# Graph attention with residual layernorm on one core: work units of one pair for both rings, or of one quad for one ring

## The chip, the core and the metric

The kernel runs on one core of one Trainium2 chip. The metric is the device time of one execution in microseconds (us); each kernel is run several times and the median is taken. Engines: TensorE (PE; its weight loads are PEld), VectorE (DVE), ScalarE (ACT), GpSimd (POOL), and SyncE (SP), which only issues DMAs here.

## The reference

```python
def reference(x, adj, W, a):          # x 8192x128 f32, adj 8192x8192 int32 (0/1, sparse, with diagonal)
    Wh = (h @ W.T).reshape(n, 4, 32).transpose(1, 0, 2)
    score_src = einsum('knd,kd->kn', Wh, a[:, :32])[:, :, None]
    score_dst = einsum('knd,kd->kn', Wh, a[:, 32:])[:, None, :]
    e = leaky_relu(score_src + score_dst, 0.2)
    e = where(adj == 0, -inf, e)
    alpha = softmax(e, axis=-1)
    h_prime = einsum('kij,kjd->kid', alpha, Wh)     # 4 heads of 32
    return layernorm(x + h_prime.transpose(1, 0, 2).reshape(n, 128))
```

## The kernel before

The exponential of a leaky ReLU is a product of one factor per row and one per column, and which of two such products holds depends only on whether the sum of the two scores is above zero. So no exponential is taken per edge. For each head a byte mask says where the sum is above zero; "edge and mask" selects the columns for the steep branch (values G), "edge exclusive-or (edge and mask)" those for the flat branch (values F). Both masks are fed to TensorE as fp8 weights, 128 columns by 128 rows at a time, and 66 columns of values (32 of data and a one for the denominator, twice: a coarse and a fine fp16 part) flow past them.

Rows are done in 16 groups of 512 (GROUPS, ROWS), the 8192 columns in 64 blocks of 128, two blocks to a pair: 32 pairs to a group (PAIRS), 512 in all. The four heads lie in two "rings" (RINGS) of two. For pair k:

- ACT and POOL make the masks of pair k (L513 to L519, L411 to L417): 4 comparisons of 128x1024, each for two groups at once (this group for one head, the next group for the other). ACT takes 2 or 3 of the 4 (2.25 on average), POOL the rest (1.75). In group 0 the masks of the other heads are made as well, in 128x512 comparisons; in the last group comparisons are 128x512. Before pair k both engines wait for the products and the exclusive or of pair k-5 (NS = 5 places, L407, L415 to L416 and their ACT twins).
- PE transposes the edges of pair k+2 into one of three PSUM banks (`transpose_edges`, L742, four transposes, AHEAD = 2, NT = 3).
- DVE does the and (`take_step`, L630) for both rings at once, 128x1024 int32 words, one operand from PSUM and one from SBUF; then the exclusive or (`take_rest`, L638) of pair k-1, the same size. The exclusive or waits until the products two before it are done (NL = 2).
- PE does 32 products with the and of pair k (`add_step`), the four transposes of pair k+2, and 32 products with the exclusive or of pair k-1 (`add_rest`), all at L754. They accumulate over a whole group in five PSUM banks; a small matmul with zeros opens a bank (L765) and another closes it (L769).

At the end of a group g the sums are finished while group g+1 runs. ACT copies the five banks to SBUF (`take_sums`, L492) after its comparisons for pair 4 of the next group (SUMS = 4). PE can open a bank for group g+1 only after its copy. POOL combines the sums in eight parts (`close`, L356 to L380) after its comparisons of the pairs in CLOSING. DVE does the reciprocal of the denominator and the layernorm statistics in `finish` (L656 to L678) from pair 16 on, POOL the inverse deviation (L384), DVE the shift (L678, `scalar_tensor_tensor` of 128x4 with both inputs in SBUF), ACT the normalisation (L498) after pair 30, and SP stores the rows.

POOL also issues the loads of edges (L337): 4 loads of 256 KB for every chunk of 8 pairs, one each after its comparisons of pairs 2, 3, 4, 5 of every eight (EDGE_UNITS), for the next chunk. The order on each engine is the order written out in its block; nothing is planned by a scheduler.

## Time and profile before

| | us |
|---|---|
| median of 3 runs | 1487.32 (1482.68 to 1493.78) |
| the profiled execution | 1484.16 |
| span in its profile | 1482.3 |
| PE, DVE, ACT, POOL busy | 1204.4, 1307.4, 1333.5, 1328.0 |

The span runs from the first to the last instruction on the core, so 1.9 us of the profiled execution lie around it. "Busy" is the time in which an engine works on at least one instruction. "Idle before" a group of instructions is the time in which their engine had nothing to do just before them, with what ended it. "issue" means that the engine waited for nothing that the profile shows.

### The profile page before, as it was taken

How to read it: one execution, taken by the hardware profiler on the slowest of the kernel's cores; microseconds unless marked ns; L12 is line 12 of the kernel's file. 1: busy time of each engine (PE TensorE's matmuls, PEld its weight loads, DVE VectorE, ACT ScalarE, POOL GpSimd, SP SyncE). 2: the span in 40 equal slices, each digit the busy share in tenths (PEclk: the TensorE clock that was granted, in tenths of full speed). 3: DMA queues.
4: the chain of work that ended last, by engine and by line, in shares of the span. 5: the costliest groups of instructions: out<-in, count | busy, mean ns of one | idle time of the engine just before them, and what ended most of it. 6: DMA issues, size and time to landing. Idle time of an engine off the chain costs nothing.

```text
span 1482.3 us, 77436 instructions
## 1 busy us (share of the span) xinstructions
PE 1204.4 (81%) x35173; PEld 1177.2 (79%) x35173; DVE 1307.4 (88%) x1422; ACT 1333.5 (90%) x1456; POOL 1328.0 (90%) x1371
## 2 busy tenths in 40 slices
PE   7047679898888889888897989889887989888985
PEld 7036669897888889788897989888887879888984
DVE  6966669899898999999798999989999889989995
ACT  2799999999999999999999999999999999999753
POOL 1788879999999999999999999999999999999854
PEclk9569989999999999999999999999999999999997
DMA  8203555657757675656746675666657665675740
GB/s 162 57 30 34 50 73 53 62 80 67 94 47 95 55 97 57 64 80 67 91 45 94 61 72 74 64 87 57 93 51 97 58 61 77 67 80 49 73 46 24
DMA packets 55842, 101.65 MB, mean 69 GB/s; under 512 B 5721, under 2 KB 18393, under 8 KB 55513
## 3 DMA queue, kind: packets, MB, share of 16 engines
q0 software_dynamic: 36864, 67.13, 52.0%
q1 hardware_dynamic: 18648, 29.56, 6.2%
q8 instruction: 277, 4.54, 1.2%
q14 instruction: 53, 0.43, 0.1%
HBM read 293.67 MB, written 4.33 MB: 201 GB/s over the span
## 4 chain that ended last, share of the span: by engine, by line
PE 45%; POOL 19%; issue 14%; ACT 11%; DVE 5%; POOLq 0%; DVEq 0%; ACTq 0%
PE bank L754 40%; POOL kept L341 14%; ACT kept L465 10%; PE bank L742 5%; DVE kept L630 3%; POOL edge L337 2%; DVE rest L638 1%; DVE shift L678 1%; POOL late L371 1%; POOL y L380 0%; ACT late L492 0%; POOL late L367 0%; POOL late L358 0%; POOL late L364 0%; POOL late L374 0%
## 5 line engine op out<-in xcount | busy, mean ns | idle before, releaser
L465 ACT ACTIVATE kept<-s_two,sd 128x1024 uint8<-128x1024 f32 (+1 forms) x1152 | 1196.5, 1116 | 87.0 <-DVE rest L638 50.1
L341 POOL TENSOR_SCALAR kept<-s_two,sd 128x1024 uint8<-128x1024 f32 (+1 forms) x896 | 967.8, 1091 | 37.0 <-DVE rest L638 19.6
L630 DVE TENSOR_TENSOR kept<-bank,kept 128x1024 int32<-128x1024 int32 x512 | 621.3, 1216 | 111.1 <-PE bank L742 79.1
L754 PE MATMUL bank<-G,kept 128*128 128x66 f16 x16384 | 600.9, 194 | 106.6 <-issue 57.9
L638 DVE TENSOR_TENSOR rest<-kept,bank 128x1024 int32<-128x1024 int32 x512 | 618.5, 1209 | 33.6 <-PE bank L754 33.4
L754 PEld LDWEIGHTS bank<-G,kept 128*128 128x128 fp8e4 x16384 | 544.4, 98 | 120.4 <-issue 64.4
L754 PE MATMUL bank<-F,rest 128*128 128x66 f16 x16384 | 595.5, 194 | 46.2 <-issue 45.7
L754 PEld LDWEIGHTS bank<-F,rest 128*128 128x128 fp8e4 x16384 | 555.4, 98 | 51.0 <-issue 50.7
L742 PE MATMUL bank<-identb,edge 128*128 128x128 bf16 x2048 | 201.9, 222 | 17.2 <-issue 9.0
L337 POOL DMA_DIRECT2D edge<-in_adj x256 | 151.5, 593 | 16.0 <-DMA kept<-in_x 16.0
L742 PEld LDWEIGHTS bank<-identb,edge 128*128 128x128 bf16 x2048 | 125.0, 98 | 24.1 <-issue 10.0
L765 PE MATMUL bank<-zeros,identb 128*128 128x2 bf16 x80 | 13.6, 169 | 80.5 <-DVE kept L630 51.3
L765 PEld LDWEIGHTS bank<-zeros,identb 128*128 128x128 bf16 x80 | 8.2, 102 | 81.7 <-issue 75.3
L341 POOL TENSOR_SCALAR kept<-y,sd 128x512 uint8<-128x512 f32 x30 | 31.6, 1053 | 19.5 <-DMA late<-sT_scratch 10.1
L356 POOL TENSOR_TENSOR late<-late 128x528 f32<-128x528 f32 x16 | 17.9, 1120 | 28.4 <-ACT late L492 28.4
L492 ACT COPY late<-bank 128x462 f32<-128x462 f32 (+1 forms) x80 | 34.1, 510 | 7.9 <-PE bank L769 7.9
L498 ACT ACTIVATE y<-y,shift,rstd 128x128 f32<-128x128 f32 x64 | 26.2, 480 | 13.1 <-DVE shift L678 13.1
L678 DVE SCALAR_TENSOR_TENSOR shift<-mv,rstd 128x4 f32<-128x4 f32 x16 | 34.0, 2123 | 1.1 <-POOL rstd L384 1.1
L341 POOL TENSOR_SCALAR kept<-late,sd 128x512 uint8<-128x512 f32 x30 | 21.7, 722 | 10.8 <-PE bank L754 7.3
L374 POOL TENSOR_TENSOR late<-late,rden 128x512 f32<-128x512 f32 x16 | 16.9, 1056 | 11.1 <-DVE rden L659 10.9
L384 POOL TENSOR_TENSOR rstd<-mv,half_t 128x4 f32<-128x4 f32 x16 | 16.7, 1043 | 11.2 <-DVE mv L673 11.2
L440 ACT COPY late<-bank 128x512 f32<-128x512 f32 x16 | 9.4, 586 | 18.9 <-PE bank L704 18.9
(77 smaller groups left out, 405.4 us busy)
## 6 DMA issues: line engine op xcount, KB each, us to landing
edge<-in_adj POOLq DMA_DIRECT2D x256, 256.0 KB, 5.3
s_two<-sT_scratch SPq DMA_DIRECT2D x30, 512.0 KB, 6.5
kept<-in_x SPq DMA_DIRECT2D x16, 256.0 KB, 6.5
y<-in_x SPq DMA_DIRECT2D x16, 256.0 KB, 7.5
out<-y SPq DMA_DIRECT2D x16, 256.0 KB, 7.2
s_two<-sT_scratch SPq DMA_DIRECT2D x2, 256.0 KB, 6.5
y<-sT_scratch SPq DMA_DIRECT2D x1, 256.0 KB, 3.7
late<-sT_scratch SPq DMA_DIRECT2D x1, 256.0 KB, 4.8
```

The source lines that it names most:

```text
L337: nc.gpsimd.dma_start(edge[:, c % NC, b], adj_v[c // (PAIRS // CP), c % (PAIRS // CP), :, b // E, b % E]).then_inc(edge_loaded[c % NC], 16)
L341: return nc.gpsimd.tensor_scalar(out, scores, STEEP, d_steep[:, j, h:h + 1], ALU.mult, ALU.add)
L356: nc.gpsimd.tensor_tensor(low, low, sums_F[:, :, HC:FC], ALU.add).then_inc(low_set, 1)
L465: return nc.scalar.activation(out, scores, ACT.Sigmoid, scale=STEEP, bias=d_steep[:, j, h:h + 1])
L492: nc.scalar.copy(late[:, b * USED:b * USED + n], acc[b][:, 0:n]).then_inc(acc_act, 1)
L498: last = nc.scalar.activation(y[:, b], y[:, b], ACT.Identity, scale=rstd[:, b:b + 1], bias=shift[:, b:b + 1])
L630: nc.vector.tensor_tensor(kept[:, :, both(k, k)[0]], edgeT[k % NT], kept[:, :, both(k, k)[0]], ALU.bitwise_and).then_inc(step_set, 1)
L638: nc.vector.tensor_tensor(rest[:, k % NL], kept[:, :, both(k, k)[0]], edgeT[k % NT], ALU.bitwise_xor).then_inc(rest_set, 1)
L678: nc.vector.scalar_tensor_tensor(shift[:, :], mv[:, :, 0], -1.0, rstd[:, :], ALU.mult, ALU.mult).then_inc(shift_set, 1)
L742: last = nc.tensor.transpose(edgeT16[k % NT][:, b * P:(b + 1) * P], edge16[:, c % NC, b, k % CP * P:(k % CP + 1) * P], identb[:, :])
L754: last = nc.tensor.matmul(acc[k][:, col:col + BC], matrices[h][:, b * P:(b + 1) * P, e], values[:, t * E + e, h].rearrange("p s c -> p (s ...
L765: nc.tensor.matmul(acc[k][:, USED:USED + 2], identb[:, :], zeros[:, :], start=True, stop=False, skip_group_check=True)
```

## The change

The unit of DVE's work becomes one ring of four column blocks (a quad, QUADS = 16 to a group) instead of both rings of two column blocks. A unit keeps its size: 128x1024 for the and and the exclusive or, 4 comparisons, 32 products. Unit k belongs to quad k // 2 and ring k % 2. What else changes:

- Order on DVE for each quad: and, and, exclusive or, exclusive or. On PE: eight transposes of quad q+2, then 32 + 32 products of the two ands, then 32 + 32 of the two exclusive ors. A transposed quad fills its bank; still three banks.
- NS = 3 quads: comparisons for unit k wait for unit k-6.
- The sums are read from PSUM by DVE: per group three `tensor_scalar` and three `tensor_tensor` adds (fine part scaled and added to the coarse), and three `tensor_reduce`. Banks 0 and 1 are closed ahead of the last two exclusive-or products and read before DVE's first and of the next group; banks 2 to 4 are read between its second and and its first exclusive or. ACT's copies go.
- Row factors: numerator and denominator share one of them, so a single `ratio` replaces alpha and beta. POOL's closing has 4 parts instead of 8; in the last group they are done by DVE.
- The shift goes from DVE (`scalar_tensor_tensor`) to POOL (a product of 128x4), with the negated mean from a DVE `tensor_scalar`.
- Loads of edges after units 1 to 4 of every eight instead of 2 to 5.

```diff
-    EDGE_UNITS = (2, 3, 4, 5)
+    EDGE_UNITS = (1, 2, 3, 4)
+    CQ = CP // U
-    NS = 5
-    PLACES = PAIRS + NS
+    NS = 3
+    PLACES = QUADS + NS
-    WORDS = ROWS * E // 4
+    WORDS = ROWS * E // 4 * U
-        CLOSING = (4, 6, 8, 10, 12, 14, 18, 20)
-        SUMS, FINISH, DEVIATION, SCALED = 4, 16, 26, 30
+        CLOSING = (7, 9, 17, 19)
+        FINISH, DEVIATION, SCALED = 12, 28, 31
...
                 if part == 0:
-                    pool.wait_ge(acc_act, done((g + 2) * BANKS))
-                    nc.gpsimd.tensor_tensor(low, low, sums_F[:, :, HC:FC], ALU.add).then_inc(low_set, 1)
+                    pool.wait_ge(acc_taken, done((g + 2) * BANKS))
+                    nc.gpsimd.tensor_tensor(sum_F, sum_F, per_row(ratio[:, g * IB:(g + 1) * IB, :], HC), ALU.mult).then_inc(low_set, 1)
                 elif part == 1:
-                    nc.gpsimd.tensor_scalar(sums_G[:, :, HC:BC], sums_G[:, :, HC:BC], 1.0 / LOW, None, ALU.mult).then_inc(top_set, 1)
+                    pool.wait_ge(low_set, g + 1)
+                    nc.gpsimd.tensor_tensor(sum_G, sum_G, sum_F, ALU.add).then_inc(top_set, 1)
...
                 nc.gpsimd.tensor_tensor(rstd[:, :], mv[:, :, 1], half_t[:, :], ALU.pow).then_inc(rstd_set, 1)
+                pool.wait_ge(rstd_set, g + 1)
+                nc.gpsimd.tensor_tensor(shift[:, :], minus_mean[:, :], rstd[:, :], ALU.mult).then_inc(shift_set, 1)
...
-                    if k >= NS:
-                        pool.wait_ge(step_done, k - NS + 1)
-                        pool.wait_ge(rest_set, k - NS + 1)
+                    q, r = quad_and_ring(k)
+                    if q >= NS:
+                        pool.wait_ge(step_done, k - RINGS * NS + 1)
+                        pool.wait_ge(rest_set, k - RINGS * NS + 1)
...
+            def take_sums(g, b):
+                dve.wait_ge(acc_done, g * BANKS + b + 1)
+                first, end = b * PER_BANK, b * PER_BANK + sums_in(b)
+                unit_of = acc[b][:, 0:(end - first) * BC].rearrange("p (k s c) -> p k s c", s=BP, c=HC)
+                n_G = max(0, min(end, CHUNKS) - first)
+                if end > CHUNKS:
+                    at = first + n_G - CHUNKS
+                    last = nc.vector.tensor_reduce(sum_F[:, at:end - CHUNKS], unit_of[:, n_G:].rearrange("p k s c -> p k c s"), AX.X, ALU.add)
+                if n_G > 0:
+                    nc.vector.tensor_scalar(sum_G[:, first:first + n_G], unit_of[:, 0:n_G, 1], 1.0 / LOW, None, ALU.mult).then_inc(small_taken, 1)
+                    dve.wait_ge(small_taken, g * BANKS_G + b + 1)
+                    last = nc.vector.tensor_tensor(sum_G[:, first:first + n_G], unit_of[:, 0:n_G, 0], sum_G[:, first:first + n_G], ALU.add)
+                last.then_inc(acc_taken, 1)
...
-                for t in range(PAIRS):
-                    take_step(pair_no(g, t))
-                    if t > 0:
-                        take_rest(pair_no(g, t - 1))
-                    if t >= FINISH and t % 2 == 0:
+                for t in range(0, PAIRS, RINGS):
+                    k = pair_no(g, t)
+                    if t == 0 and g > 0:
+                        take_sums(g - 1, 0)
+                        take_sums(g - 1, 1)
+                    for r in range(RINGS):
+                        take_step(k + r)
+                    if t == 0 and g > 0:
+                        for b in range(2, BANKS):
+                            take_sums(g - 1, b)
+                    for r in range(RINGS):
+                        take_rest(k + r)
+                    if t >= FINISH:
                         next(closing, None)
...
-                for t in range(PAIRS):
-                    k = pair_no(g, t)
-                    add_step(g, t)
-                    if t > 0:
-                        pe.wait_ge(rest_set, k)
-                    if k + AHEAD < GROUPS * PAIRS:
-                        transpose_edges(k + AHEAD)
-                    if t > 0:
-                        add_rest(g, t - 1)
+                for t in range(0, PAIRS, RINGS):
+                    q = pair_no(g, t) // RINGS
+                    if q + AHEAD < GROUPS * QUADS:
+                        transpose_edges(q + AHEAD)
+                    for r in range(RINGS):
+                        add_step(t + r)
+                    if t + RINGS == PAIRS:
+                        for b in range(CHUNKS // PER_BANK):
+                            close_bank(b)
+                    for r in range(RINGS):
+                        add_rest(t + r)
+                for b in range(CHUNKS // PER_BANK, BANKS):
+                    close_bank(b)
```

In the setup five small DVE operations (three of 128x256 for alpha and beta, a copy, a negation) and their two scalings make way for one `tensor_scalar`, and two exponentials on ACT for one.

## Rows read from the trace of the kernel before

**Rows 1.** Windows: length, busy PE, PEld, DVE, ACT, POOL, PE clock, DMA share, GB/s

```profile
209.29:1384.63 1175.34, 1021.63 (x30604) 1002.86 (x30605) 1079.72 (x1063) 1115.10 (x1135) 1130.00 (x1134) 0.98 0.64 72
1384.63:1464.30 79.67, 72.54 (x2178) 71.16 (x2178) 72.91 (x75) 45.00 (x73) 47.88 (x66) 0.98 0.45 47
```

**Rows 2.** Who waited for whom in 209.29 to 1384.63 (us, times, longest us)

```profile
PE bank L754 <- issue: 96.5, 74, 3.5
DVE kept L630 <- PE bank L742: 55.5, 38, 6.8
DVE rest L638 <- PE bank L754: 32.3, 34, 2.5
PE bank L765 <- ACT late L492: 29.0, 14, 6.7
PE bank L754 <- DVE kept L630: 20.8, 22, 2.1
```

**Rows 3.** Timeline of PE, one place (start us, us; bracket: idle before)

```profile
725.07 0.64 PE L754 MATMUL bank<-G,kept 128*128 128x66 f16 x16 [2.14 <-issue]
...
726.74 1.12 PE L754 MATMUL bank<-G,kept 128*128 128x66 f16 x32
727.70 0.38 PE L742 MATMUL bank<-identb,edge 128*128 128x128 bf16 x4
727.92 0.77 PE L754 MATMUL bank<-F,rest 128*128 128x66 f16 x20
```

**Rows 4.** DMA queue of instructions, whole span: packets, MB, share of 16 engines

```profile
q8 instruction: 277, 4.54, 1.2%
```

**Rows 5.** Groups of instructions, 209.29 to 1384.63: busy us, mean ns | idle before

```profile
L678 DVE SCALAR_TENSOR_TENSOR shift<-mv,rstd 128x4 f32<-128x4 f32 x14 | 33.7, 2404 | 0.0
L492 ACT COPY late<-bank 128x462 f32<-128x462 f32 (+1 forms) x71 | 30.3, 510 | 0.0
L358 POOL TENSOR_SCALAR late<-late 128x528 f32<-128x528 f32 x14 | 21.8, 1560 | 0.0
L364 POOL TENSOR_TENSOR late<-late 128x528 f32<-128x528 f32 x14 | 15.9, 1137 | 0.4
L356 POOL TENSOR_TENSOR late<-late 128x528 f32<-128x528 f32 x14 | 15.7, 1121 | 16.6 <-ACT late L492 16.6
L367 POOL TENSOR_TENSOR late<-late,alpha 128x528 f32<-128x528 f32 x14 | 15.4, 1103 | 0.4
```

**Rows 6.** Timeline of DVE: around the shift of one group, and the shift of group 14

```profile
441.84 2.41 DVE L678 SCALAR_TENSOR_TENSOR shift<-mv,rstd 128x4 f32<-128x4 f32 x1
444.17 1.21 DVE L630 TENSOR_TENSOR kept<-bank,kept 128x1024 int32<-128x1024 int32 x1
445.31 1.20 DVE L638 TENSOR_TENSOR rest<-kept,bank 128x1024 int32<-128x1024 int32 x1
...
1450.46 0.15 DVE L678 SCALAR_TENSOR_TENSOR shift<-mv,rstd 128x4 f32<-128x4 f32 x1
```

**Rows 7.** Groups of instructions by form, whole span: nearest kin of the added operations

```profile
L604 DVE TENSOR_TENSOR late<-bank,G 128x396 f32<-128x396 f32 x21 | 11.7, 557 | 0.0
L555 DVE TENSOR_REDUCE wh_part<-bank 128x1 f32<-128x256 f32 x32 | 13.1, 411 | 0.0
L384 POOL TENSOR_TENSOR rstd<-mv,half_t 128x4 f32<-128x4 f32 x16 | 16.7, 1043 | 11.2 <-DVE mv L673 11.2
```

**Rows 8.** Setup, timeline of DVE: one of the operations that go

```profile
38.79 0.42 DVE L572 SCALAR_TENSOR_TENSOR beta<-alpha,beta 128x256 f32<-128x256 f32 x1
```

**Rows 9.** Timeline of the tail after the last bank is closed

```profile
1464.14 0.17 PE L769 MATMUL bank<-zeros,identb 128*128 128x2 bf16 x1
...
1475.20 0.87 DVE L664 BATCH_NORM_STATS2 stats<-y 128x6 f32<-128x128 f32 x4 [2.42 <-POOL y L380]
```

**Rows 10.** Edge loads: last load of a chunk; landing times in 209.29 to 1384.63

```profile
715.57 0.60 POOL L337 DMA_DIRECT2D edge<-in_adj  x1
...
DMA to landing us min/median/max: 4.9/5.3/8.5
```

More of the change, by code:

```diff
@@ L484, in _ @@
             second_part(UNITS - 1)
-            def take_sums(g):
-                act.wait_ge(var_set, done(g))
-                for b in range(BANKS):
-                    n = sums_in(b) * BC
-                    act.wait_ge(acc_done, g * BANKS + b + 1)
-                    nc.scalar.copy(late[:, b * USED:b * USED + n], acc[b][:, 0:n]).then_inc(acc_act, 1)
             def normalise(g):
@@ L693, in _ @@
+            nc.vector.tensor_tensor(rows_y, rows_y, sum_G[:, :, 0:D_OUT], ALU.add).then_inc(sum_set, 1)
+            for _ in closing:
                 pass
@@ L746, in add_pair @@
[L746 to L759 removed]
+                if q >= NT:
+                    pe.wait_ge(rest_set, RINGS * (q - NT + 1))
@@ L770, in close_bank, with two_heads @@
                                  skip_group_check=True).then_inc(acc_done, 1)
-            def by_head(g, k):
-                older, newer = places(k)
-                kept_first = both(k, k)[1]
+            def two_heads(g, q):
+                older, newer = places(q)
+                kept_first = both(q, q)[1]
                 two = [(newer, int(kept_first)), (older, int(not kept_first))]
-                two = two if g % 2 == 0 else two[::-1]
-                return [(r, place, side) for r in range(RINGS) for place, side in two]
@@ L791, in group @@
[L791 to L802 removed]
+                return two if g % 2 == 0 else two[::-1]
```

245 lines of the change are left out of this document (118 added, 127 removed).

## The prediction

> **What bounds the kernel now.** I read the share of busy time first, then cut the span at the openings of the accumulation banks, since these mark the groups. Group 0 ends with the opening at 209.29, group 15 begins with that at 1384.63, so groups 1 to 14 take 1175.34 / 14 = 83.95 us each; group 15 takes 79.67 and the tail after it 18.0 (to 1482.3) [rows 1]. The first 209.3 us are setup and group 0, where ACT is busy without a gap because it makes two sets of masks; a change in the products gains nothing there.
>
> Per group, in groups 1 to 14 [rows 1]: POOL is busy 1130.00 / 14 = 80.7, ACT 79.7, DVE 77.1, PE 73.0. POOL alone would be named as the bound. The waits correct this. PE stands still for another 96.5 / 14 = 6.9 us per group with "issue" as the reason, 74 times [rows 2], in the middle of a run of like products [rows 3]. That looks like instructions that come late: 277 packets of 4.54 MB [rows 4] are 16 KB each, and PE's 70,000 instructions are the bulk of them. Apart from that PE waits 29.0 us for ACT's copies of the sums and 20.8 us for ands [rows 2], 49.8 / 14 = 3.55 per group. Taking these off, PE needs 83.95 - 3.55 = 80.4 us a group by itself. Group 15 confirms it: ACT and POOL have half their work there and DVE is busy 72.91 us, yet the group takes 79.67 [rows 1]. So POOL (80.7), PE (80.4 with its late instructions) and ACT (79.7) are all within 5% of the period, and DVE loses (55.5 + 32.3) / 14 = 6.3 us waiting for PE [rows 2]. Relieving one engine is worth little; the change relieves three and loads the fourth.
>
> **POOL.** Four of eight closing parts go. Their kinds: 1.121 + 1.560 + 1.137 + 1.103 = 4.9 us per group [rows 5]. Added is the shift, 128x4. The nearest row is the power of the same size, 1.04 [rows 7]; below, nothing. I take 0.5, since a power should be dearer than a product. POOL: 80.7 - 4.9 + 0.5 = 76.3.
>
> **ACT.** 30.3 / 14 = 2.2 us of copies go [rows 5]: 77.5.
>
> **DVE.** The shift goes: 33.7 / 14 = 2.4 us [rows 5]. Its place in the timeline shows that this is a wait in disguise: 2.41 us beside a busy POOL, 0.15 us for the same operation when POOL is nearly idle [rows 6]. A tiny `tensor_scalar` comes, about 0.1. The sums come: per group three scalings and three adds of 231, 231 and 66 elements, and three reductions that read 330, 462 and 264. The and is 1024 elements in 1.14 us from start to start [rows 6], 1.11 ns an element all in; an add of 396 elements with one input from PSUM takes 0.557 alone and a reduction of 256 takes 0.411 [rows 7]. At about 1.04 ns an element, the slope between those two, (0.557 - 0.411) / 140, elements are 2112 x 1.04 = 2.2 us; nine operations at 0.07 (1.14 less 1024 x 1.04 ns) are 0.6; three waits of an add for its own scaling, 0.15 each (0.411 - 256 x 1.04 ns is what a lone one takes beyond its elements), 0.45. Sum 3.3 us. From below 2.2 (the elements alone); from above 9 x 0.557 = 5.0. DVE: 77.1 - 2.4 + 0.1 + 3.3 = 78.1.
>
> At one point the Trainium skill (SBUF — State Buffer, Who interferes with whom) bears on this. It says that a VectorE instruction contends with GpSimd if it has two inputs in SBUF or runs in a two-port mode, and that the loser waits for the whole instruction; the two numbers of the shift agree with it. By that rule the new adds, with one input in PSUM, wait for nobody. The ands, of the same kind, follow each other at 1.14 us with POOL busy [rows 6], so row and rule agree, and the case in which they do not is a rival below.
>
> **PE.** The number and size of products and transposes stay, and so, I take it, do the late instructions: 80.4. What changes is what PE waits for. The 29.0 us for ACT's copies go, and most of the 20.8 us for ands, of which each group's share follows the blocked shift; together 3.55 per group, less 0.2 that I leave. At the boundary there is a new wait. Count from the end of the last ands' products: DVE reads banks 0 and 1 (four operations, about 1.5 us), then does its first and (1.14), 2.7 in all with the handing over, while PE has two runs of 32 products, 0.96 each from start to start, and eight transposes, 0.44 at 0.22 for four [rows 3]: waits 0.35. The second and costs another 0.15. Then DVE reads banks 2 to 4 (1.8 us) and does the exclusive or (1.14), while PE has one run (0.96): waits 1.9. With 0.1 for the last, PE waits up to 2.5 us at each boundary. None of it is added where PE lags (then DVE is ahead except for the reads of banks 0 and 1, which follow PE's closing), and during such a wait instructions can arrive that would else be late. Bounds 0 and 2.5; I take 1.4.
>
> **Transposes at the head of a quad.** The same number, eight at once. Before, DVE's and waited for them 55.5 us in all [rows 2], since PE does pair k+2's only after the products of k and after the exclusive or of k-1. Now those of quad q+2 are done a full quad ahead, so this reason for DVE to wait goes; next late is the exclusive or, which needs its buffer two units back. In DVE's pace that is 3 x 1.14 us after PE could begin on it, less 0.96 for the run: 2.4 us of slack, about as before. So PE's late instructions of up to 3.5 us [rows 2] still reach DVE. I give this edit nothing of its own; its ends are 0 and the 55.5 / 14 = 4.0 us per group (if it were all gain).
>
> **Six units of lead instead of five.** Comparisons wait on the exclusive or six units back, nine DVE operations (10 us) ahead of use, against six before (7 us). This smooths ACT and POOL, which are now 1 to 4 us under the period anyway. It is in the 0.2 above.
>
> **The sum.** Middle groups: 80.4 + 0.2 + 1.4 = 82.0, against 83.95: -1.95 x 14 = -27. DVE (78.1), ACT and POOL lie below, so they set nothing by themselves; but DVE's own margin shrinks, and I leave the gain at that. Group 0 to 1: PE waited 6.7 us for ACT, which was late with its first masks (the longest of that row, [rows 2]); now about 2.5: -4. Group 15: its DVE is busy 72.9, with the sums of group 14 76 us; PE's boundary wait adds +1. Setup: three operations like the one shown go, 0.42 each, with a copy, a negation and two scalings of 0.2 to 0.35, one comes, all on DVE, which is the busy engine there [rows 8]: -1.7. Tail: from the last closing at 1464.14 to 1475.20 POOL and DVE take 11.1 us [rows 9]. After: the rest of the reads (2.2, since DVE starts them before PE has ended), multiply and add of 528 (0.62 each by the same slope, 1.3 with a wait), reciprocal (0.5), two of 512 (1.25): 5.3. The shift on POOL adds 0.3. Tail -5.5.
>
> -27 - 4 + 1 - 1.7 - 5.5 = -37. The profiled execution took 1484.16, so 1447; the median of the runs shown is 1487.32, 3.2 higher, within their spread of 11. I predict 1447, 1484.16 - 37, and let the 3 us stand in the range.
>
> **Rivals.**
>
> (a) DVE sets the pace. If instructions come late only where PE would wait anyway, PE needs 73.0 + a little, and DVE's 78.1 plus some 1.5 of unevenness is the period: 79.6, another 2.4 x 14 = 34 us less: 1413. For it: four engines had 3 us between the fullest and the period before, and three get lighter. Against: group 15 took 79.67 with DVE at 72.9. The Trainium skill (Runtime: NRT & Kernel Launch, Instruction fetch mechanics) says that blocks of 16 KiB are fetched while the last one runs and that this is mostly hidden, which would give this case; the packets' size agrees, the 96.5 us of idle do not.
>
> (b) PE sets the pace and the boundary wait counts in full, with its clock falling in it now and then: 80.4 + 2.5 + 0.6 = 83.5, middle groups gain 0.45 x 14 = 6, so 1447 + 21 = 1468. For it: 80.4 hardly moves. Against: waits and late instructions can overlap.
>
> (c) The other side: edges come late. PE needs a chunk two pairs earlier than before (transposes of quad q+2 at the head of quad q) and POOL issues its last load only one unit earlier. Before, the last load of a chunk was issued at 715.57 [rows 10] and first used at 727.70 [rows 3]; less 5.3 to landing [rows 10], 6.8 us were left. Two pairs earlier are 5.2 us, the two runs that stood ahead of those transposes another 2.3, and the earlier issue gives 2.6 back: some 1.9 us are left, and landings reach 8.5 [rows 10]. If PE waits at each of the four chunks of a group, 15 x 4 = 60 waits, the gain of 37 is used up at 0.6 us each; at 1.5 us it is 1447 + 90 = 1537, at 1.0 us 1507. For it: the small margin. Against: POOL, no longer the fullest engine and with one unit more of lead, issues about 2.6 us earlier relative to PE.
>
> (d) The adds and scalings on DVE are blocked by POOL as the shift was, 6 x 2.25 = 13 us per group at worst, half of that if only the adds are: + 6.7 x 15 = 100, 1547.
>
> **How the numbers follow.** The forecast 0.55, with a range of its own of 1430 to 1458; (a) 0.17, (b) 0.16, (c) 0.06, (d) 0.03, and 0.03 for something unseen that leaves it as it was. A measurement of this kernel tells about 1% from no change, 15 us: faster means under 1472. That holds for the forecast, (a) and nearly all of (b), 0.85; within 1% get 0.07, slower 0.08. The range goes from 1420, inside (a), to 1472, past (b).
>
> **What would show it.** Right: openings of banks no longer wait for ACT, and the gaps between openings of bank 0 are 81 to 83 us; DVE's share of busy time rises to about 93% between them; waits of ands for transposes nearly gone; nine new DVE operations of 3.3 us together per group; POOL and ACT each with more idle time; the tail 12 to 13 us. Wrong: "issue" waits of PE that shrink (then a), or grow; PE waiting for edges at heads of quads (c); adds of over 1 us on DVE (d); a period above 83.

## The result, and the profile after

| | before | after |
|---|---|---|
| median, us | 1486.59 (1482.68 to 1493.78) | 1412.2 (1408.97 to 1417.19) |
| profiled execution / its span, us | 1484.16 / 1482.3 | 1412.29 / 1410.2 |
| busy PE, DVE, ACT, POOL, us | 1204.4, 1307.4, 1333.5, 1328.0 | 1204.7, 1329.6, 1284.4, 1247.2 |

The ratio is 0.9497 [0.9451, 0.9543]: 5.0% faster. Forecast were 1447 us and a range of 1420 to 1472; the time lies below both. It is the time of rival (a), 1413, in which DVE sets the pace and PE's late instructions don't count.

Cut at the openings of the banks as in [rows 1], the windows of after are these: groups 1 to 14, group 15, and one middle group by itself (columns as in rows 1).

```profile
201.60:1317.66 1116.06, 1018.74 (x30604) 988.42 (x30605) 1100.17 (x1193) 1078.21 (x1072) 1064.82 (x1093) 1.00 0.67 76
1317.66:1397.42 79.76, 71.24 (x2161) 69.40 (x2160) 74.17 (x80) 38.68 (x62) 41.56 (x60) 0.99 0.37 39
682.86:761.50 78.64, 71.86 (x2186) 70.15 (x2187) 78.44 (x86) 76.67 (x77) 76.35 (x80) 1.00 0.69 77
```

A middle group takes 1116.06 / 14 = 79.72 us instead of 83.95. DVE is busy 1100.17 / 14 = 78.6 of it, and in the single group 78.44 of 78.64. Eight of the fourteen groups take 78.6 to 78.9, the other six 79.3 to 82.0. PE's busy time per group is what it was, 72.8 against 73.0.

| stretch | before | after | difference | forecast |
|---|---|---|---|---|
| until group 1 opens | 209.29 | 201.60 | -7.7 | -4 - 1.7 |
| groups 1 to 14 | 1175.34 | 1116.06 | -59.3 | -27 |
| group 15 | 79.67 | 79.76 | +0.1 | +1 |
| tail, to the end of the span | 18.0 | 12.8 | -5.2 | -5.5 |

The four differences sum to -72.1, the difference of the spans. All but a few us of the surprise lie in the middle groups. Who waited for whom there, in 201.60 to 1317.66 (us in all, times, longest):

```profile
PE bank L770 <- issue: 44.7, 51, 2.2
PE bank L770 <- DVE rest L615: 21.5, 16, 1.6
PE bank L770 <- DVE kept L606: 15.6, 13, 1.5
DVE rest L615 <- PE bank L770: 11.2, 16, 1.8
...
PE bank L779 <- DVE kept L606: 7.1, 12, 1.0
```

Two more rows of the same view are PE's waits for edges, 4.8 us in 7 times, and 2.6 us of issue at the transposes. They are read against [rows 2] and these lines of before. The first two are of the same view, the third is from the timeline of PE:

```profile
PE bank L742 <- issue: 9.0, 5, 2.6
PE bank L742 <- DVE rest L638: 1.3, 1, 1.3
...
209.29 0.16 PE L765 MATMUL bank<-zeros,identb 128*128 128x2 bf16 x1 [6.68 <-ACT late L492]
```

PE's "issue" idle falls from (96.5 + 9.0) / 14 = 105.5 / 14 = 7.5 us per group to 47.3 / 14 = 3.4. Of the 29.0 us for ACT in before, 6.68 lie ahead of 209.29, in group 0, so its waits for other engines were (22.3 + 20.8 + 1.3) / 14 = 3.2 per group. In after, waits for other engines and for edges are (21.5 + 15.6 + 7.1 + 4.8) / 14 = 3.5. So on PE's side 73.0 + 7.5 + 3.2 = 83.7 of the 83.95 has become 72.8 + 3.4 + 3.5 = 79.7. The waits did not fall, they are now for DVE; what fell is the idle time called issue, the late instructions, which the forecast held fixed. On DVE's side, waits for PE fall from (55.5 + 32.3) / 14 = 6.3 to 0.9.

The groups of instructions that answer to [rows 5] and [rows 7], same stretch (busy us, mean ns | idle before):

```profile
L606 DVE TENSOR_TENSOR kept<-bank,kept 128x1024 int32<-128x1024 int32 x449 | 525.6, 1210 | 0.5
L615 DVE TENSOR_TENSOR rest<-kept,bank 128x1024 int32<-128x1024 int32 x448 | 523.9, 1208 | 11.5 <-PE bank L770 11.2
...
L626 DVE TENSOR_REDUCE late<-bank 128x165 f32<-128x330 f32 (+2 forms) x43 | 20.9, 514 | 0.3 <-PE bank L783 0.3
L663 DVE TENSOR_SCALAR mv<-mv 128x4 f32<-128x4 f32 x14 | 16.8, 1203 | 0.5
...
L630 DVE TENSOR_TENSOR late<-bank,late 128x231 f32<-128x231 f32 (+1 forms) x42 | 14.3, 341 | 1.4
L628 DVE TENSOR_SCALAR late<-bank 128x231 f32<-128x231 f32 (+1 forms) x43 | 14.1, 327 | 1.1 <-PE bank L783 1.1
...
L664 DVE TENSOR_SCALAR minus_mean<-mv 128x4 f32<-128x4 f32 x14 | 3.1, 222 | 0.0
L380 POOL TENSOR_TENSOR shift<-minus_mean,rstd 128x4 f32<-128x4 f32 x14 | 2.8, 203 | 1.1
```

The ands wait for nothing any more (0.5 us in all). The sums cost (20.9 + 14.3 + 14.1) / 14 = 3.5 us per group, forecast 3.3. But L663, the addition of epsilon to four variances, takes 1203 ns here. Before, the same operation took 170 ns:

```profile
L673 DVE TENSOR_SCALAR mv<-mv 128x4 f32<-128x4 f32 x14 | 2.4, 170 | 0.5
```

One boundary, first PE, then DVE (start us, us; bracket: idle before):

```profile
759.95 0.61 PE L756 MATMUL bank<-identb,edge 128*128 128x128 bf16 x8
761.50 0.18 PE L779 MATMUL bank<-zeros,identb 128*128 128x2 bf16 x1 [0.95 <-DVE kept L606]
...
765.45 0.54 PE L770 MATMUL bank<-F,rest 128*128 128x66 f16 x12 [1.57 <-DVE rest L615]
```

```profile
756.50 2.33 DVE L615 TENSOR_TENSOR rest<-kept,bank 128x1024 int32<-128x1024 int32 x2
758.76 0.38 DVE L628 TENSOR_SCALAR late<-bank 128x231 f32<-128x231 f32 x1
759.18 0.40 DVE L630 TENSOR_TENSOR late<-bank,late 128x231 f32<-128x231 f32 x1
...
760.23 2.34 DVE L606 TENSOR_TENSOR kept<-bank,kept 128x1024 int32<-128x1024 int32 x2
```

PE waits 0.95 + 1.57 = 2.5 us, the upper end of the forecast's bounds. It costs nothing by itself: DVE works through the boundary without a gap, and DVE is the one that is late. What the boundary costs is DVE's 3.5 us.

### The profile page after: what moved, and what is told of

Read it like the earlier page. It is cut to its first block, busy times and chain, and to the rows that moved or that the text cites. A ratio compares the mean times of both kernels' runs of the same rounds, so it can differ in the third digit from the quotient of the medians.

```text
span 1410.2 us, 76980 instructions
## 1 busy us (share of the span) xinstructions
PE 1204.7 (85%) x35173; PEld 1167.1 (83%) x35173; DVE 1329.6 (94%) x1564; ACT 1284.4 (91%) x1375; POOL 1247.2 (88%) x1319
## 4 chain that ended last, share of the span: by engine, by line
PE 34%; issue 19%; DVE 15%; ACT 14%; POOL 11%; DMA 2%; DVEq 0%; POOLq 0%; ACTq 0%
PE bank L770 30%; ACT kept L456 14%; POOL kept L350 9%; DVE rest L615 8%; DVE kept L606 4%; PE bank L756 3%; DMA edge<-in_adj 2%; POOL edge L346 1%; DVE late L626 1%; DVE late L628 1%; DVE late L630 0%; POOL y L374 0%; DVE stats L655 0%; DVE mv L660 0%; DVEq L605 0%
## 5 line engine op out<-in xcount | busy, mean ns | idle before, releaser
L606 DVE TENSOR_TENSOR kept<-bank,kept 128x1024 int32<-128x1024 int32 x512 | 600.8, 1211 | 41.7 <-issue 30.3
L770 PE MATMUL bank<-G,kept 128*128 128x66 f16 x16384 | 555.5, 193 | 72.9 <-DVE kept L606 43.3
L615 DVE TENSOR_TENSOR rest<-kept,bank 128x1024 int32<-128x1024 int32 x512 | 598.9, 1208 | 17.0 <-PE bank L770 16.7
L770 PE MATMUL bank<-F,rest 128*128 128x66 f16 x16384 | 569.8, 194 | 44.8 <-issue 23.3
L770 PEld LDWEIGHTS bank<-F,rest 128*128 128x128 fp8e4 x16384 | 527.6, 98 | 65.5 <-issue 26.5
L756 PE MATMUL bank<-identb,edge 128*128 128x128 bf16 x2048 | 158.1, 220 | 54.2 <-ACT G L453 43.4
L573 DVE TENSOR_TENSOR bank<-G,s_two 128x396 f32<-128x396 f32 (+1 forms) x44 | 25.1, 616 | 0.0
L456 ACT ACTIVATE kept<-late,sd 128x512 uint8<-128x512 f32 x35 | 24.3, 715 | 0.0
L626 DVE TENSOR_REDUCE late<-bank 128x165 f32<-128x330 f32 (+2 forms) x48 | 23.4, 514 | 0.3 <-PE bank L783 0.3
L456 ACT ACTIVATE kept<-y,sd 128x512 uint8<-128x512 f32 x33 | 22.9, 714 | 0.0
```

What stands on the lines that cost most here:

```text
L456: return nc.scalar.activation(out, scores, ACT.Sigmoid, scale=STEEP, bias=d_steep[:, j, h:h + 1])
L573: last = nc.vector.tensor_tensor(to[m % NU][:, 0:n], Wh[:, blk], v[:, blk, :].unsqueeze(3).to_broadcast([P, n, HEADS, HC]), ALU.mult)
L606: nc.vector.tensor_tensor(kept[:, r, both(q, q)[0]], edgeT[q % NT], kept[:, r, both(q, q)[0]], ALU.bitwise_and).then_inc(step_set, 1)
L615: nc.vector.tensor_tensor(rest[:, k % NL], kept[:, r, both(q, q)[0]], edgeT[q % NT], ALU.bitwise_xor).then_inc(rest_set, 1)
L626: last = nc.vector.tensor_reduce(sum_F[:, at:end - CHUNKS], unit_of[:, n_G:].rearrange("p k s c -> p k c s"), AX.X, ALU.add)
L756: last = nc.tensor.transpose(edgeT16[q % NT][:, (u * IB + b) * P:(u * IB + b + 1) * P], edge16[:, c % NC, b, at:at + P], identb[:, :])
```

## The experiments

Each is an edit of before or of after, or of an earlier experiment; e1, e2 and so on are their numbers. Ratios are to runs of before on the same chip. Where a stretch of 210 to 1290 us is named, all kernels are in their middle groups there.

**1 and 2. Closing without quads, quads without closing.** The change has two halves that can be parted: the unit of work, and who finishes the sums.

```diff
 # e1: before, with the closing of after
-        CLOSING = (4, 6, 8, 10, 12, 14, 18, 20)
+        CLOSING = (7, 9, 17, 19)
+                    if t == 0 and g > 0:
+                        take_sums(g - 1, 0)
+                        take_sums(g - 1, 1)
                     take_step(pair_no(g, t))
...
 # e2: after, with ACT's copies and POOL's eight parts of before
-        CLOSING = (7, 9, 17, 19)
+        CLOSING = (4, 6, 8, 10, 12, 14, 18, 20)
-        FINISH, DEVIATION, SCALED = 12, 28, 31
+        SUMS, FINISH, DEVIATION, SCALED = 4, 16, 26, 31
```

In e2 the row factor that after no longer has is replaced by a product with ones, so that the eight parts stay eight.

> Pairs as units, order and places as before; only the closing of after: DVE reads the sums, four closing parts on GpSimd, shift on GpSimd. Theory A (the offload makes the gain, because GpSimd, ScalarE and the copies of the sums held the period and VectorE is now the pace): within 10 us of the changed kernel, 1412 to 1425. Theory B (the order in quads makes it: VectorE no longer waits for transposes and TensorE's late instructions are absorbed): little is gained, 1460 to 1480, and VectorE still waits some 5 us a group for TensorE. Theory C (both are needed, since each leaves one engine at 80 to 81 us a group): 1435 to 1455.

> Quads as units and the order of after; the sums are copied by ScalarE, closed in eight parts by GpSimd (one of them a product with ones in place of the removed factor), shift on VectorE, as before. Theory A: little is gained, 1465 to 1487. Theory B: most of it, 1415 to 1435. Theory C: GpSimd's 80.7 us a group are the floor, 1440 to 1465.

Measured: e1 1477.27 us, 0.9929 [0.99, 0.9957]; e2 1565.56, 1.0513 [1.0469, 1.0557]. The new closing alone brings 10 us, as little as theory B expected, and its middle groups still take 83.89. In 210 to 1290 its PE has 98.4 us of issue idle, as before (99.5). e2 is 79 us slower, outside all three ranges, and this row of its waits in 210 to 1300 says why (with POOL's 57.0 us for the variances and ACT's 54.2 for the shift beside it):

```profile
PE bank L748 <- DMA edge<-in_adj: 74.3, 29, 3.7
```

Edges come late, and closing steps wait for one another, at points that were chosen for a lead of five units. In e11 the same kernel has its parts moved to fit a lead of six units (two counts of steps in DVE's `finish` go with it):

```diff
-        CLOSING = (4, 6, 8, 10, 12, 14, 18, 20)
-        SUMS, FINISH, DEVIATION, SCALED = 4, 16, 26, 31
+        CLOSING = (5, 6, 7, 8, 9, 10, 18, 20)
+        SUMS, FINISH, DEVIATION, SCALED = 4, 10, 27, 31
...
```

> Quads with the old closing as in the second experiment, but with its steps placed for the longer lead (GpSimd's parts after units 5 to 10, 18, 20; VectorE's finish from unit 10; GpSimd's deviation after unit 27), so that no closing step waits for the other engine. If only the misplaced waits made the second experiment slow: 1450 to 1470, with GpSimd's 80.7 us a group as the floor. If GpSimd as the fullest engine, late with its edge loads, is what makes quads slow: 1490 or more, with TensorE waiting for edges 3 us a group or more.

Measured: 1511.88, 1.0164 [1.0127, 1.0201]. 54 of the 79 us go with the placing alone, but quads with the old closing stay slower than before. PE still waits 18.4 us for edges in 210 to 1300. So neither half explains the 72 us by itself, and what each is worth depends on something third.

**3. The shift back on DVE.** With it POOL's step for the inverse deviation goes back to its old place, after unit 26.

```diff
-        FINISH, DEVIATION, SCALED = 12, 28, 31
+        FINISH, DEVIATION, SCALED = 12, 26, 31
...
-                nc.gpsimd.tensor_tensor(shift[:, :], minus_mean[:, :], rstd[:, :], ALU.mult).then_inc(shift_set, 1)
...
-                nc.vector.tensor_scalar(minus_mean[:, :], mv[:, :, 0], -1.0, None, ALU.mult).then_inc(var_set, 1)
...
+                nc.vector.scalar_tensor_tensor(shift[:, :], mv[:, :, 0], -1.0, rstd[:, :], ALU.mult, ALU.mult
+                                               ).then_inc(shift_set, 1)
```

> The changed kernel with only the shift back on VectorE (two inputs in SBUF, blocked by GpSimd as before). Theory A and C (VectorE sets the pace in the changed kernel): the blocked 2.4 us a group less 0.2 for the negation, some 2.0 x 15 = 30 us more than after, 1435 to 1445. If another engine sets the pace: less than 10 us more, 1412 to 1422.

Measured: 1414.98, 0.9506 [0.9455, 0.9558], no difference to after. Expected were 1435 to 1445 if DVE sets the pace. The rows show why that does not follow (210 to 1290 of e3):

```profile
L666 DVE SCALAR_TENSOR_TENSOR shift<-mv,rstd 128x4 f32<-128x4 f32 x13 | 14.9, 1145 | 0.0
...
L661 DVE TENSOR_SCALAR mv<-mv 128x4 f32<-128x4 f32 x13 | 2.2, 170 | 0.4
```

The shift is blocked by POOL, L661 isn't: POOL comes to its own step early and stands still for L661 (24.1 us in 13 times). In after it is the other way round: the shift is off DVE, POOL's step comes after unit 28, and L663 takes 1203 ns while POOL is comparing. DVE's cost is 1145 + 170 against 1203 + 222 ns per group, so e3 takes no work off DVE and puts none on it, and it can't tell whether DVE sets the pace. Nor does it part the move of the shift from the move of POOL's step: together they removed one blocked operation and made another.

**4. Loads of edges at their old place.**

```diff
-    EDGE_UNITS = (1, 2, 3, 4)
+    EDGE_UNITS = (2, 3, 4, 5)
```

> The changed kernel with the loads of edges after units 2 to 5 of every eight as before. If the new place of the loads is why TensorE's late instructions fell from 7.5 to 3.4 us a group, they rise again to 6 or more and the time to 1425 to 1440. If it is the pace (TensorE has to wait for VectorE anyway): they stay near 3.4; TensorE waits for edges at the heads of more quads, at 0.5 to 1.5 us each, part of it absorbed: 1412 to 1430.

Measured: 1462.14, 0.9845 [0.9801, 0.9888]: 50 us of the 74 are gone with this one line, more than either range allowed. Its rows, 210 to 1290:

```profile
PE bank L770 <- issue: 60.2, 57, 2.8
...
PE bank L756 <- DMA edge<-in_adj: 40.9, 14, 5.2
```

Two things return: PE waits for edges at one chunk in each group (40.9 us), and its late instructions grow (60.2 + 3.7 against 45.5 in after). This run does not say what each of the two costs.

**5 to 7. The same loads with a sixteenth of the bytes.** Number and place of the loads stay. Most columns keep edges of the first chunks, so the sums are other sums; the work on every engine is the same.

```diff
-                nc.gpsimd.dma_start(edge[:, c % NC, b], adj_v[..., b // E, b % E]
+                w = CHUNK if c < NC else CHUNK // 16
+                nc.gpsimd.dma_start(edge[:, c % NC, b, 0:w], adj_v[..., b // E, b % E, 0:w]
```

> The kernel before, but from the third chunk on only a sixteenth of each edge load is transferred (the other columns keep old edges, so those parts of the adjacency are left out); every instruction and issue stays. If TensorE's late instructions are fetches held up by the edge transfers, its issue idle falls from 7.5 us a group to under 1, VectorE's waits for it fall too, and GpSimd's 80.7 us is what is left: 81.5 us a group, some 1440 to 1455. If the idle has another cause: unchanged, 1480 to 1490.

> The changed kernel with the same cut of the edge transfers. VectorE is busy 78.6 us a group and paces it: 78.6 to 78.9 in every group, 1385 to 1400 in all, so late instructions and late edges together cost the changed kernel some 15 to 25 us. If something else than VectorE paces it: under 1385.

> Pairs as units with the closing of after (the first experiment), with the same cut of the edge transfers. If what the quads bring on top of the new closing is only that TensorE's late instructions reach VectorE less, the two forms are alike without them: within 8 us of the changed kernel with small transfers. If the order of pairs costs VectorE time in itself: 20 us or more above it.

| | all bytes | 1/16 of the bytes | issue idle in 210 to 1290 |
|---|---|---|---|
| before | 1486.59 | 1462.0 (e5), 0.9804 [0.9743, 0.9866] | 99.5 -> 12.6 |
| before with the new closing | 1477.27 (e1) | 1413.14 (e7), 0.9475 [0.9411, 0.9539] | 98.4 -> 9.8 |
| after | 1412.2 | 1392.3 (e6), 0.9336 [0.9266, 0.9406] | 45.5 -> 4.6 |

The issue idle goes almost wholly when the edge traffic goes. So it is neither a property of PE nor of the instruction stream alone, it is what the edge loads do to the stream.

The packets in the traces show the step between. In before, PE has 75 issue waits in 210 to 1290. Each ends 1.2 to 1.9 us after the end of a packet of 16 KB on the instruction queue, no two after the same packet; in after it is 1.2 to 1.6 us for all 53. At a random moment of before the last such packet ended 1.2 to 1.9 us ago in some 15 of 100 cases. In the 1.5 us before these packets began, 14 packets of edge loads were in flight on average in before and 15 in after, against 7 and 8.5 before the other instruction packets. So the instructions do come late, and they come late while the 16 DMA engines are full of edges.

e5 is above its range of 1440 to 1455: PE still waits 33.5 us for ACT's copies, and DVE 21.7 us for POOL. Without the edge traffic the new closing is worth 1462.0 - 1413.1 = 49 us, and quads another 21. DVE waits for PE in neither e6 nor e7, yet e7's middle groups take 79.76 us and e6's 78.59. The difference lies in small operations with both ends in SBUF: 2.9 us per group in e7 against 1.7 in e6, most of it in this row of e7 (1272 ns in e6):

```profile
L652 DVE TENSOR_SCALAR mv<-mv 128x4 f32<-128x4 f32 x13 | 29.0, 2230 | 0.4
```

In e6 DVE has nothing left to wait for (210 to 1290; the third busy time is DVE's, 1077.22 of 1080):

```profile
210.00:1290.00 1080.00, 1018.63 (x30091) 976.07 (x30087) 1077.22 (x1168) 1058.52 (x1050) 1049.33 (x1075) 1.00 0.14 26
```

**8. The transposes back between the products.** This undoes the part that the change is named for.

```diff
-                    if q + AHEAD < GROUPS * QUADS:
-                        transpose_edges(q + AHEAD)
                     for r in range(RINGS):
                         add_step(t + r)
+                    if q + AHEAD < GROUPS * QUADS:
+                        transpose_edges(q + AHEAD)
```

> The changed kernel with the eight transposes of quad q+2 between the products of the ands and those of the exclusive ors instead of at the head. VectorE-paced theory: TensorE does the same work, VectorE sees no difference; TensorE needs a chunk of edges 2 us later, so it waits for no edges: 1408 to 1416. If the place at the head matters: 1420 to 1435, with VectorE waiting longer for exclusive-or buffers, since 1.8 us of transposes at half clock or 0.44 at full clock stand ahead of them.

Measured: 1416.42, 0.9509 [0.9444, 0.9575]; after 1412.2. The intervals overlap, and a middle group takes 79.99 against 79.72. Two units' products later, PE no longer waits for edges (4.8 us in after), and ands still don't wait for transposes. The place at the head is worth nothing that these runs can tell. (Eight transposes took 1.03 us at a granted clock of 0.5, 1.2 GHz, at 83.5 us of after, not the 1.8 that the expectation has.)

**9 and 10. Comparisons and mask operations at half width.** From group 3 on half of the rows keep stale masks (the comparisons for them begin a group earlier); PE's work stays. The ands and exclusive ors, not shown in the cut below, are halved in the same way. This was meant to leave PE alone with its instructions in either order.

```diff
-                            last = compare(kept_u8[:, r, two, u, :, e], ...
+                            w = ROWS if g < 2 else ROWS // 2
+                            last = compare(kept_u8[:, r, two, u, 0:w, e], ...
```

> Pairs with the new closing; from group 3 on the ands, exclusive ors and comparisons cover only half of each tile (half of the masks is left stale), while TensorE's stream and all transfers stay whole. So TensorE alone paces groups 4 to 14. Theory S (TensorE's own pace is the same in both forms, and quads only keep its late instructions from VectorE): 79 to 81 us a group in both forms, issue idle 7 to 8. Theory F (fewer instructions come late when the products come in the order of quads): 80 here, 76 to 77 in the quads.

> The changed kernel with the same halving from group 3 on. Theory S: 79 to 81 us a group, issue idle of TensorE 7 to 8 us a group, as in pairs. Theory F: 76 to 77 us a group and issue idle of 3 to 4, as in the changed kernel.

Measured, one run each: 1460.37 and 1433.4. PE's issue idle in 450 to 1290 is 92.8 + 8.9 us in pairs and 89.2 + 4.2 (and 2.3 where banks open and close) in quads, some 10 and 9 us per group: more than in either whole kernel, in both orders. Neither theory allowed for that. The likely reason is on POOL: half as long comparisons bring the loads closer together, and the median landing over the whole span rises from 5.3 us in before to 6.4 and 6.1. The two kernels don't part pairs from quads; but they gave the idea that the next five test.

**How close the loads stand.** A chunk's four loads follow POOL's comparisons of four successive units. Where t mod 4 is 1, ACT takes three comparisons and POOL one, so from the load before to the load of such a unit there are 1.7 us, where other gaps are 2.8 or more. Places 1 to 4 begin with a short unit and have none inside; places 2 to 5 and 0 to 3 have one. In before, closing parts behind the comparisons of units 4, 12 and 20 widen three of the four. Counted in POOL's timeline, gaps under 2.5 us are, per group: before 1.0, e1 2.1, e4 3.0, e12 4.0, e10 5.8, e9 8.4, and none in after, e2, e3, e8, e11, e13, e14 and e16. By the share of the queue in the page, a load takes the 16 DMA engines 0.520 x 1482.3 / 256 = 3.0 us. Below, POOL's loads of one chunk in e12 and in e14 (described next): gaps of 1.7, 4.1, 2.8 in the one and 2.9, 2.8, 2.8 in the other.

```profile
713.89 0.60 POOL L347 DMA_DIRECT2D edge<-in_adj  x1
715.61 0.58 POOL L347 DMA_DIRECT2D edge<-in_adj  x1
719.70 0.60 POOL L347 DMA_DIRECT2D edge<-in_adj  x1
722.52 0.58 POOL L347 DMA_DIRECT2D edge<-in_adj  x1
```

```profile
723.74 0.58 POOL L347 DMA_DIRECT2D edge<-in_adj  x1
726.66 0.58 POOL L347 DMA_DIRECT2D edge<-in_adj  x1
729.45 0.58 POOL L347 DMA_DIRECT2D edge<-in_adj  x1
732.24 0.58 POOL L347 DMA_DIRECT2D edge<-in_adj  x1
```

**11 and 12. Small layernorm operations on POOL, with loads at 0 to 3 (e12) and at 1 to 4 (e14).** The diff is to after; e14 has it without its last two lines.

```diff
-                nc.vector.tensor_scalar(mv[:, :, 1], mv[:, :, 1], EPS, None, ALU.add)
-                nc.vector.tensor_scalar(minus_mean[:, :], mv[:, :, 0], -1.0, None, ALU.mult).then_inc(var_set, 1)
...
+                nc.gpsimd.tensor_scalar(mv[:, :, 1], mv[:, :, 1], EPS, None, ALU.add).then_inc(small_set, 1)
+                nc.gpsimd.tensor_scalar(minus_mean[:, :], mv[:, :, 0], -1.0, None, ALU.mult)
...
-    EDGE_UNITS = (1, 2, 3, 4)
+    EDGE_UNITS = (0, 1, 2, 3)
```

> Meant to be faster than the changed kernel: the two small layernorm operations (variance plus epsilon, negated mean) go from VectorE to GpSimd, and edges are loaded after units 0 to 3 of every eight. VectorE loses 1.43 us a group, GpSimd gains 0.4. VectorE-paced theory: 78.6 - 1.4 = 77.2 a group where nothing else holds, and no waits for edges: 1412 - 20 - 5 = 1385 to 1397. If another engine paces: 1405 or more.

> The changed kernel with only the two small layernorm operations moved from VectorE to GpSimd; edges after units 1 to 4 as in the changed kernel. Theory G: the loss of the twelfth experiment came from its loads (units 0 to 3, one gap of 1.7 us in each four), so this one gains what was meant there: 77.2 to 78.5 us a group, 1388 to 1402. If the small operations themselves did it: 1430 or more.

Measured: e12 1457.1, 0.9764 [0.969, 0.9837]; e14 1404.79, 0.9457 [0.941, 0.9504]. The two differ in nothing but the place of the loads, by one unit, and by 52 us. Nobody waits for edges in e12. Its issue idle is this, in 210 to 1290 (e12, then e14):

```profile
PE bank L771 <- issue: 127.0, 94, 3.1
```

```profile
PE bank L771 <- issue: 48.4, 52, 1.7
```

and e12's loads land after 6.9 us, e14's after 5.2 (medians). e12 was meant to be faster and missed; e14 lies just above its 1388 to 1402 and has the lowest median of all kernels with all the edges. Its DVE does 1.4 us less per group (L663 and L664), and its middle groups take 78.5 against 79.72, 1.2 less, as it should be where DVE sets the pace. But these stage times are from its fastest execution, 1396.78, and the gain over after, 7 us in the medians, is less than the intervals can tell from nothing.

**13, 15 and 16. The spacing of loads by itself.**

```diff
 # e13: e1 with           e16: before with
-    EDGE_UNITS = (2, 3, 4, 5)
+    EDGE_UNITS = (1, 2, 3, 4)
...
 # e15: after, loads two at once
-    EDGE_UNITS = (1, 2, 3, 4)
+    EDGE_UNITS = (1, 3)
-                        load_edges(k // CP + 1, EDGE_UNITS.index(t % CP))
+                        for b in ((0, 1) if t % CP == 1 else (2, 3)):
+                            load_edges(k // CP + 1, b)
```

> The first experiment (pairs, new closing) with one edit: edges are loaded after units 1 to 4 of every eight instead of 2 to 5, so that no gap between two loads holds only one comparison of GpSimd. Theory G (late instructions come from edge loads issued less than their 3.0 us of transfer apart; the quads themselves bring little): issue idle of TensorE falls from 7.5 to about 4 us a group, 80 to 81 us a group, 1412 to 1430. Theory Q (the order in quads keeps late instructions from VectorE): little change, 1465 to 1480.

> The changed kernel with its four edge loads of a chunk issued two after unit 1 and two after unit 3; same number and size, the last one a unit earlier, so no wait for edges is added. Theory G: half of the gaps are 0.6 us, landings rise from 5.2 to 7 us or more, TensorE's issue idle from 3.4 to 8 or more us a group, 1440 to 1480. If spacing does not matter: 1408 to 1418.

> The kernel before with edges after units 1 to 4 instead of 2 to 5. Theory G: its one short gap a group goes, issue idle falls from 7.5 to about 5; GpSimd at 80.7 us a group stays the floor, so 82.5 to 83 us a group, 1465 to 1478. Otherwise: 1483 to 1492.

| | loads at 2 to 5 | loads at 1 to 4 | issue idle in 210 to 1290 |
|---|---|---|---|
| before | 1486.59 | 1470.69 (e16), 0.9894 [0.9871, 0.9918] | 99.5 -> 44.2 |
| pairs, new closing | 1477.27 (e1) | 1441.9 (e13), 0.9697 [0.9666, 0.9728] | 98.4 -> 73.8 |
| quads, new closing | 1462.14 (e4) | 1412.2 (after) | 63.9 -> 45.5 |

e15 takes 1483.97, 0.9982 [0.9951, 1.0013]. That is 72 us more than after, all but 3 us of the gain, with the same instructions on PE, DVE and ACT. Its loads stand as close as they can, two in one row of POOL's timeline:

```profile
704.46 1.12 POOL L346 DMA_DIRECT2D edge<-in_adj  x2
721.64 1.14 POOL L346 DMA_DIRECT2D edge<-in_adj  x2
```

The loads of a pair are in flight together; 137.0 us of issue idle in 210 to 1290, landing after 6.8. So closeness costs, without any other change, and spacing pays in all three pairs of the table: 16, 35 and 50 us (the last with 40.9 us of waits for edges in it, which later loads bring as well, so this pair alone would not show it).

e13 is also the link between the two halves. It lies between its two ranges: the spacing did not make pairs as fast as quads, as theory G had it. With the loads spaced, the new closing is worth 1470.7 - 1441.9 = 29 us and quads another 30. These are the windows 210 to 1290 of e16 and e13, where DVE's busy time rises from 1001.96 to 1051.38 and POOL's and ACT's fall:

```profile
210.00:1290.00 1080.00, 962.72 (x28483) 941.01 (x28481) 1001.96 (x989) 1041.93 (x1057) 1055.39 (x1054) 0.97 0.64 73
```

```profile
210.00:1290.00 1080.00, 953.76 (x28826) 933.62 (x28823) 1051.38 (x1117) 1015.46 (x1001) 1004.79 (x1027) 0.99 0.65 74
```

What pairs still lose to quads can be read on DVE. e13's middle groups take 82.1 us, 2.4 more than after's. Its small operations with both ends in SBUF are blocked for longer (L651 below at 1835 ns; 3.2 us per group with L635 and L652, against 1.7 for the three in after), and it waits for PE 1.9 us per group against 0.9.

```profile
L651 DVE TENSOR_SCALAR mv<-mv 128x4 f32<-128x4 f32 x13 | 23.8, 1835 | 0.4
...
L635 DVE TENSOR_SCALAR rden<-late 128x16 f32<-128x16 f32 x13 | 12.0, 923 | 0.0
...
L652 DVE TENSOR_SCALAR minus_mean<-mv 128x4 f32<-128x4 f32 x13 | 5.9, 455 | 0.0
```

That is an account of 2.5 us out of rows, not a test: no run changed the order of units and kept these two fixed. The first of them is what e7 and e6 differ in as well, so most of what quads bring there may hang on where the small operations meet POOL's work, and not on the order of the products. That stays open.

## Why the prediction was wrong, step by step

**The step that failed** is "The number and size of products and transposes stay, and so, I take it, do the late instructions: 80.4." Their number did stay. The 6.9 us of issue idle per group (7.5 with the transposes) were taken for a property of PE's 70,000 instructions. They belong to the edge loads: with 1/16 of their bytes 99.5 us of before become 12.6 (e5), with spaced loads 44.2 (e16), and with loads in twos the 45.5 of after become 137.0 (e15). The change moved the loads by one unit, and the prediction priced that move only as time in hand for the last load ("the earlier issue gives 2.6 back"), never as a change of the gaps between loads. On PE's side this term came out 4.1 us per group lower than the forecast had it, and the waits higher: 3.5 us instead of 0.2 + 1.4. Together that is 2.3 x 14 = 32 us, which is what the 59.3 of the middle groups have over the 27. The gain that was forecast, fewer waits of PE, did not come.

**But it isn't the gain by itself.** e16 halves the late instructions in the kernel before and brings 16 us: its PE then waits 36.5 us for ACT's copies and its DVE 18.1 for POOL's comparisons, with POOL busy 1055 of 1080. And e1 relieves POOL and ACT and brings 10, since late instructions remain. Only together do they leave DVE as the one bound. The sentence "relieving one engine is worth little; the change relieves three and loads the fourth" was right, and its consequence was rival (a).

**Rival (a)** had the price right: a period of 79.6 and 1413 us; it came to 79.72 and 1412.2. Its condition, "if instructions come late only where PE would wait anyway", was put wrongly: 3.4 us per group still come late, and in part where PE would not have waited. What holds is that less of it comes late, and that DVE hardly feels the rest (0.9 us of waits). Part of the nearness is luck: no row gave the 1.5 us of unevenness that DVE's 78.1 was raised by, and the rest of the sum had -4 - 1.7 + 1 - 5.5 where -7.7, +0.1 and -5.2 came. The argument against it, group 15 taking 79.67 with DVE at 72.9, was a fact about a group with comparisons half as long. Its loads stand closer, with gaps of 1.95 to 2.5 us among them in both kernels, and PE's issue idle is 7.0 us there before and 8.6 after. It still takes 79.76, and so it never spoke about the others. The Trainium skill (Runtime: NRT & Kernel Launch, Instruction fetch mechanics) has crossing a block "mostly hidden". The runs put a condition on it: true without the edge traffic (4.6 us in 1080 in e6), not with it (45.5 in after, 137.0 in e15).

**DVE, 78.1:** measured 78.6. The sums were forecast at 3.3 and took 3.5, from the slope of two rows. The shift's 2.4 went, but "a tiny `tensor_scalar`, about 0.1" took 0.22, and the one that had been there all along went from 0.17 to 1.20, because POOL, with its own step after unit 28 instead of 26, no longer stands still for it. The Trainium skill (SBUF — State Buffer, Who interferes with whom) was cited for the adds, where it held: 341 ns beside a busy POOL, with one input in PSUM. The same section names `tensor_scalar` among the operations that can take a two-port mode, and so would also have spoken about L663, whose input and output lie in SBUF, had it been asked of every operation left and not of the new ones alone. By the rows of after and e13 this is 1.2 to 1.8 us a time.

**POOL and ACT, 76.3 and 77.5:** measured 1064.82 / 14 = 76.1 and 77.0. The shift on POOL was taken at 0.5 and took 0.20; the power beside it takes 1.04.

**PE's waits:** the 6.68 us ahead of 209.29 were counted twice, in the 3.55 per group and in the -4 of group 0 to 1; without them PE by itself is 80.9, not 80.4. The wait at the boundary was counted at up to 2.5 us, and 0.95 + 1.57 us stand in the timeline. It was then added to the period at 1.4, which it isn't: a wait for the bound engine is slack, not cost.

**Transposes at the head:** costed at nothing of their own, bounds 0 and 4.0. e8 shows nothing that can be told, within some 4 us in all. DVE's waits for transposes went as forecast, from 55.5 us to none.

**Group 0 to 1, setup and tail:** -5.7 forecast and -7.7 measured ahead of group 1, since PE's wait there fell from 6.68 to 0.33 us and not to 2.5; -5.5 and -5.2 in the tail. The tail's steps cost a little more than their price of 0.62 each: the two of 528 elements 0.71 us each, the two of 512 0.69.

**Rivals (b) to (d):** (b) fell with the fixed 80.4. (c) was near: PE waits for edges 4.8 us in all, in 7 waits of up to 1.1, so the 1.9 us in hand were nearly enough, and e4, a single unit later, shows the mechanism with 14 waits of up to 5.2 us. Yet even that is no case of "slower": it ends at 1462. (d) did not occur for the adds; it did, at small size, for the leftover operations.

## What to carry to other kernels

Idle time with "issue" as its reason is no fixed property of the engine that shows it. Look at what else the DMA engines carry in that moment, and at the gaps between the loads, before it is carried into a sum as a constant. A load moved by one unit can matter through its neighbours more than through its own deadline, and here the same four loads at other places were worth between 16 and 72 us. Where several engines lie within 5% of the period, price a change from the busy time of whichever is left fullest, and ask what it will still wait for: the period was 1.1 us above the fullest engine in after, 1.9 in e16 and 3.2 in before. And when an engine stops waiting for another, ask which small operations it will now run beside.

## What was not expected of the hardware

- In these kernels late instructions grow when large loads stand close. PE's issue idle in 1080 us was 4.6 us with small loads (e6), 45.5 with loads 2.8 us or more apart (after), 134.5 with one gap of 1.7 in each four (e12, all lines together), 137.0 with two at once (e15), while the bytes moved stay within a few per cent (e6 aside). Before the packet that ends such a wait began, 15 packets of edge loads were in flight on average in e15 and 3 before the others, 14 and 3.5 in e12. That instruction packets queue behind the loads' packets is the reading that fits; on which engine they meet isn't shown. Nor do the gaps settle it alone: e1 has twice as many short ones as before and the same idle, e4 three times as many and less (63.9 against 99.5), and e16 and e13, with none, have 44.2 and 73.8. What else weighs in stays open.
- A 128x4 `tensor_scalar` on DVE with both ends in SBUF took 170 ns where POOL stood still (e3) and 928 (e1), 1203 (after) and 1835 (e13) on average where POOL was comparing or issuing a load. The seven longest in e13, 2.5 to 2.9 us, each lasted until two comparisons of POOL that had begun after them were done. DVE's operations of 231 and 66 elements with an input in PSUM took 327 to 341 ns in all these kernels.
- On POOL a power of 128x4 took 1.04 us and a product of the same size 0.20.
